# Rows sorted by pair of experts: one send, tiles of both experts, residual and norm on the sorted rows, one scatter to the output

## The reference

```python
logits = jnp.einsum('btd,ed->bte', x, Wr)
probs = jax.nn.softmax(logits / TEMPERATURE, axis=-1)
topk_vals, topk_idx = jax.lax.top_k(probs, TOPK)                  # TOPK = 2
router_weights = topk_vals / topk_vals.sum(-1, keepdims=True)
gate = jnp.einsum('btk,btke->bte', router_weights, one_hot)
h = jax.nn.silu(jnp.einsum('btd,efd->btef', x, W1))               # W1: 8 x 512 x 128
y = jnp.einsum('btef,edf->bted', h, W2)                           # W2: 8 x 128 x 512
out = jnp.einsum('bte,bted->btd', gate, y)
...
x = _layernorm(x + out, axis=-1)
```

## Time and profile before

| | us |
|---|---|
| three timed runs | 1376.46, 1378.03, 1380.54 |
| median | 1378.03 |
| the profiled execution, its own time | 1379.32 |
| its span, first to last instruction | 1377.4 |
| end of cross attention, about | 748 |
| first scatter issued / last scatter issued | 800.26 / 961.8 |
| first and last matmul of the experts | 845.34 / 1329.86 |

### The profile page before, as it was taken

One profiled execution on the slowest core, in us unless ns is written; L12 is line 12 of the kernel. 1 busy time (PEld: TensorE's weight loads), 2 busy tenths in 40 slices (PEclk: granted clock), 3 DMA queues, 4 the chain that ended last, 5 costly groups with the idle time before them and its releaser, 6 DMA issues.

```text
span 1377.4 us, 30644 instructions
## 1 busy us (share of the span) xinstructions
PE 962.4 (70%) x10082; PEld 815.0 (59%) x10083; DVE 857.2 (62%) x2598; ACT 729.5 (53%) x1364; POOL 445.7 (32%) x535
## 2 busy tenths in 40 slices
PE   4888888884999999999997402111698977676740
PEld 2777777773888888888886301000587866555530
DVE  3688888885788888888885730000454666566552
ACT  3666766653776767767763300000575765555531
POOL 3123333332010010010102357777002055654555
PEclk8989998887999999999997555555799999899985
DMA  6930000000001000000000002111233334443431
GB/s 193 290 87 15 15 15 15 15 9 18 13 11 21 10 11 17 10 19 10 0 1 1 1 38 71 51 59 52 55 93 86 92 95 106 99 107 99 101 87 53
DMA packets 157233, 73.72 MB, mean 54 GB/s; under 512 B 76034, under 2 KB 151042, under 8 KB 157188
## 3 DMA queue, kind: packets, MB, share of 16 engines
q1 hardware_dynamic: 148996, 56.34, 15.6%
q0 software_dynamic: 8192, 16.79, 4.2%
HBM read 22.76 MB, written 37.75 MB: 44 GB/s over the span
## 4 chain that ended last, share of the span: by engine, by line
PE 38%; DVE 22%; issue 21%; ACT 13%; another core or an unknown queue 2%; POOL 2%; DMA 1%; DVEq 1%; ACTq 0%; SPq 0%; POOLq 0%
PE bank L449 9%; PE bank L451 8%; PE bank L450 8%; PE bank L551 4%; DVE at L925 4%; DVE X L1002 3%; ACT XTa L746 3%; DVE mx L909 3%; ACT qzh L746 3%; PE bank L537 3%; PE bank L528 2%; DVE st L992 2%; ACT vz_self L755 1%; DVE z L937 1%
## 5 line engine op out<-in xcount | busy, mean ns | idle before, releaser
L424 POOL DMA_INDIRECT wst<-yd,pos x128 | 129.9, 1015 | 222.2 <-DVE z L1117 105.6
L449 PE MATMUL bank<-XTa,qzh 128*128 128x128 f16 x768 | 146.0, 226 | 37.7 <-ACT XTa L746 37.7
L925 DVE TENSOR_TENSOR at<-bank,rc 64x32 f32<-64x32 f32 (+1 forms) x768 | 153.5, 200 | 14.4
L831 ACT ACTIVATE pr<-bank 128x512 f32<-128x512 f32 x96 | 57.3, 597 | 192.4 <-remote 106.5
L760 ACT ACTIVATE pr<-bank 128x512 f32<-128x512 f32 x192 | 114.1, 594 | 79.5 <-PE bank L528 78.3
L909 DVE TENSOR_REDUCE mx<-bank 128x8 bf16<-128x512 f32 x192 | 132.9, 692 | 28.7 <-PE bank L451 23.1
L451 PE MATMUL bank<-XTa,qzl 128*128 128x128 f16 x768 | 146.5, 226 | 0.0
L450 PE MATMUL bank<-XTa,qzh 128*128 128x128 f16 x768 | 146.3, 226 | 0.0
L764 ACT ACTIVATE pt<-bank 128x512 f32<-128x512 f32 x192 | 113.3, 590 | 60.5 <-PE bank L537 60.1
L411 POOL DMA_INDIRECT xd<-XTa,pos x128 | 123.8, 968 | 65.3 <-issue 65.3
L1098 DVE TENSOR_TENSOR xtl<-xs,xth 128x512 f16<-128x512 f32 x96 | 66.4, 695 | 120.4 <-ACT xth L832 71.5
(11 more groups left out here) (202 smaller groups left out, 3084.5 us busy)
## 6 DMA issues: line engine op xcount, KB each, us to landing
yd<-at SPq DMA_DIRECT2D x96, 128.0 KB
xd<-blank SPq DMA_DIRECT2D x2, 3072.0 KB, 20.7
X<-x_dram SPq DMA_DIRECT2D x16, 256.0 KB, 2.8
wst<-w_dram SPq DMA_DIRECT2D x16, 256.0 KB, 2.7
xd<-blank SPq DMA_DIRECT2D x1, 4096.0 KB, 28.3
cin<-ctx_in_dram SPq DMA_DIRECT2D x16, 256.0 KB, 2.8
out_dram<-z SPq DMA_DIRECT2D x16, 256.0 KB
xd<-blank SPq DMA_DIRECT2D x1, 2048.0 KB, 21.5
```

The costliest lines, as they stand in the source:

```text
L424: nc.gpsimd.indirect_dma_start(out=yg[k][:, t, :], out_offset=None, in_=yd[chunk_of(n)], in_offset=bass.IndirectOffsetOnAxis(ap=pos[k][:, ...
L449: nc.tensor.matmul(out_, lh, rh, start=start, stop=False, **kw)
L831: nc.scalar.activation(s32[n % 4][:], bank[n % 4][:], ACT.Silu, scale=IWS)
L925: m = nc.vector.tensor_tensor(dst, src, r, ALU.mult)
```

## The change

Each row has an unordered pair of experts, one of 28. Rows are now sorted by pair, not by expert, into 92 tiles of 128 rows (64 full ones and room for 28 remainders, rounded up to a multiple of four). A row is sent once, with its two gates and its token number behind it (264 halves, 528 bytes). Each tile is put through both experts of its pair: `up` and `down` take an expert index e in place of the half c, with four hidden blocks each and 128 rows moving. The results of both experts lie in one PSUM bank; DVE adds them, times the gates that travelled along, onto the residual row that POOL rebuilt from its halves (`mix`), takes the statistics, and POOL applies the norm and scatters the rows straight to the output by token number (`give`); padding rows carry the number 8192 and are dropped. The stores to yd, the gathers, the four chunks, DVE's copies, ACT's share of the norm and the last 13 groups' finish behind PE are gone. SP waits for all 64 sends before its first load.

The core of the diff:

```diff
+PAIRS = [(a, b) for a in range(E) for b in range(a + 1, E)]
+NP = len(PAIRS)
+NTILE = 4 * ((TOK // P + NP - 1 + 3) // 4)
+PB = NP // 4 * NT
+ROW = 2 * D + 8
...
+            for n in range(NT // SEG):
+                sp.wait_ge(sent[n], 16 * SEG)
...
-                for t in range(t0, t1):
-                    for k in range(2):
-                        nc.gpsimd.indirect_dma_start(out=xd[chunk_of(t)], out_offset=bass.IndirectOffsetOnAxis(ap=pos[k][:, t:t + 1], axis=0),
-                                                     in_=xhl[:, t, :], in_offset=None).then_inc(sent[n], 16)
+            for t in range(NT):
+                if t % SEG == 0 and t >= 2 * SEG:
+                    pool.wait_ge(sent[t // SEG - 2], 16 * SEG)
+                nc.gpsimd.indirect_dma_start(out=xd, out_offset=bass.IndirectOffsetOnAxis(ap=pos[:, t:t + 1], axis=0),
+                                             in_=rows_out[:, t, :], in_offset=None).then_inc(sent[t // SEG], 16)
+            def take(j, i):
+                wait_apart(pool, ld_r[i], 8 * (j - i) + 16, pool_ready, POOL_READY)
+                nc.gpsimd.tensor_tensor(zr[i], row16[i][:, :, 0:D], row16[i][:, :, D:2 * D], ALU.add).then_inc(f_xs, 1)
+                nc.gpsimd.tensor_copy(held[:, i, :], row_token[i]).then_inc(f_id, 1)
+            def give(j, i, more):
+                inv_std(j, f_ag, 2 * G, f_rs)
...
+                    nc.gpsimd.tensor_scalar(zo[k], zr[i][:, k, :], mv[:, k, 0:1], rstd[:, k:k + 1], ALU.subtract, ALU.mult).then_inc(f_fin, 1)
...
+                for k in range(4):
+                    nc.gpsimd.indirect_dma_start(out=out_rows, out_offset=bass.IndirectOffsetOnAxis(ap=dest[:, k:k + 1], axis=0), in_=zo[k],
+                                                 in_offset=None, bounds_check=TOK - 1, oob_is_err=False).then_inc(put[k], 16)
+                if more:
+                    take(j + 2, i)
...
-            def up(k, c, base):
-                n = 2 * (k % 2) + c
-                for h in range(2):
-                    w = base + (2 * c + h) * 2 * P
-                    m = three(H[n][:, h * RT:(h + 1) * RT], (W1[:, bass.ds(w, P)], W1[:, bass.ds(w + P, P)]),
+            def up(q, e, base):
+                r = slice(q % 2 * P, q % 2 * P + P)
+                for f in range(FC):
+                    w = base[e] + f * 2 * P
+                    m = three(H[(2 * q + e) % 4][:, f * P:(f + 1) * P], (W1[:, bass.ds(w, P)], W1[:, bass.ds(w + P, P)]),
...
-                    for r in range(2):
-                        q = slice(h * RT + r * P, h * RT + (r + 1) * P)
-                        m = three(Y[k % 2][:, r * P:(r + 1) * P], (sh[n][:, q], sl[n][:, q]), (W2[:, bass.ds(w, P)], W2[:, bass.ds(w + P, P)]),
+                for f in range(FC):
+                    w = base[e] + f * 2 * P
+                    c = slice(f * P, (f + 1) * P)
+                    m = three(Y[q % 4][:, e * P:(e + 1) * P], (sh[n][:, c], sl[n][:, c]), (W2[:, bass.ds(w, P)], W2[:, bass.ds(w + P, P)]),
...
+            nc.vector.tensor_tensor(M16.rearrange("p (c t) -> p c t", t=NT), rt[:, 0].unsqueeze(1).to_broadcast([P, NP, NT]),
+                                    code.unsqueeze(2).to_broadcast([P, NP, NT]), ALU.is_equal).then_inc(r_m, 1)
...
+            for n in range(4):
+                b = slice(n * PB, (n + 1) * PB)
+                dve.wait_ge(r_rank, n + 1)
+                link(nc.vector.tensor_tensor_scan(runs[:, b], wipe[:, b], bank[4 + n][:, 0:PB], 0.0, ALU.mult, ALU.add))
...
+                link(nc.vector.tensor_tensor(runs[:, b], runs[:, b], bank[n][:, 0:PB], ALU.add))
...
+            link(nc.vector.scalar_tensor_tensor(out=runs_c, in0=start.unsqueeze(2).to_broadcast([P, NP, NT]), scalar=float(P), in1=runs_c,
+                                                op0=ALU.mult, op1=ALU.add))
+            link(nc.vector.tensor_tensor(runs, runs, M16, ALU.mult))
+            link(nc.vector.tensor_reduce(rt[:, 0], runs.rearrange("p (c t) -> p t c", t=NT), AX.X, ALU.add))
...
+            def mix(i, q, e):
...
+                nc.vector.scalar_tensor_tensor(out=z4, in0=bank[4 + q % 4][:, e * P:(e + 1) * P], scalar=row_gate[q // 4][:, q % 4, e:e + 1],
+                                               in1=z4, op0=ALU.mult, op1=ALU.add).then_inc(f_z if e else f_a, 1)
```

More of the change, by code:

```diff
@@ L316, in _ @@
+            for n in range(NT // SEG):
+                sp.wait_ge(sent[n], 16 * SEG)
+            for k in range(2):
+                load(k, k)
+            load_rows(0, 0)
+            for k in range(2, 4):
+                load(k, k)
+            load_rows(1, 1)
+            turn(0, 0)
+            with sp.Fori(0, (NJ - 3) // 2) as j:
+                turn(2 * j + 1, 1)
+                turn(2 * j + 2, 0)
         @block.gpsimd
@@ L427, in _ @@
[L427 to L441 removed]
+            pool.wait_ge(r_id, 1)
@@ L444, in _ @@
+            nc.gpsimd.memset(dest[:], 0).then_inc(f_fin, 4)
+            take(0, 0)
+            take(1, 1)
+            give(0, 0, True)
+            with pool.Fori(0, (NJ - 3) // 2) as j:
+                give(2 * j + 1, 1, True)
+                give(2 * j + 2, 0, True)
+            give(NJ - 2, 1, False)
+            give(NJ - 1, 0, False)
+            for k in range(4):
+                pool.wait_ge(put[k], 16 * NJ)
         @block.tensor
@@ L692, in four @@
                         if follow:
[L693 to L696 removed]
+                            up((q + 1) % 8, e, ahead)
+                        if k == 1 and e == 0 and not last:
+                            pe.reg_mov(pairs, load_word(j + 1))
+                        down(i, q, e, base)
                     base = ahead
[L699 to L700 removed]
@@ new lines, in _ @@
+            runs_c = runs.rearrange("p (c t) -> p c t", t=NT)
+            nc.vector.tensor_scalar(over[:], runs_c[:, :, NT - 1], lane_rows, None, ALU.is_gt).then_inc(r_ov, 1)
+            dve.wait_ge(r_ov, 1)
+            for n in range(4):
+                b = slice(n * PB, (n + 1) * PB)
+                link(nc.vector.tensor_tensor(runs[:, b], runs[:, b], bank[n][:, 0:PB], ALU.add))
+            dve.wait_ge(r_nt, 1)
+            nt, cum, start, ones_c = (small[:, n * NP:(n + 1) * NP] for n in range(4))
@@ new lines, in turn @@
+                    if k == 2 and not start:
+                        dve.wait_ge(f_ag, j)
+                    if k > 1 or not start:
+                        spread(i - 2, (q + 6) % 8)
+                    if k > 0 or not start:
+                        mix(i - 1, (q + 7) % 8, 1)
+                    if k == 1 and not start:
+                        moments(j - 1)
+            turn(0, 0)
+            with dve.Fori(0, (NJ - 1) // 2) as j:
+                turn(2 * j + 1, 1)
+                turn(2 * j + 2, 0)
```

451 lines of the change are left out of this document (174 added, 277 removed).

## The result

| | before | after |
|---|---|---|
| median of 11 runs, us | 1381.05 | 1371.4 |
| lowest to highest, us | 1376.46 to 1390.51 | 1365.83 to 1374.14 |
| span of the profiled execution, us | 1377.4 | 1366.2 |

The ratio is 0.9907 (95% interval 0.9884 to 0.9929): 0.9% faster, just clear of what can't be told from nothing. The forecast was 1377, its own range 1362 to 1392. But the time came about differently than forecast, and the kernel before turned out to have two times, 1381 and 1226, depending on the chip that it ran on.

What follows compares the result with a forecast made beforehand. PE's sequencer was taken to bound the expert loop: 896.1 + 23 x 19.2 = 1337.7, plus 23 stutter, 13 tail, 2.5 slow start and clock = 1376.3; adjusted for time outside the span and run offset, 1377 us, range 1335 to 1425.

Steps and rivals of the forecast that it cites:

- stutter in the loop: Expert loop: PE's issue gaps behind each turn's burst of four scatters, 1.05 us for 22 bursts, +23, bounds 0 to 47.
- slow start, clock: Expert start and loop: 1.5 us for PE's slow start plus 1 for the granted clock, +2.5 in all.
- Router and sends: Before the experts: router +10.3 us, first scatter at 810.6, 64 scatters 1.266 apart, first matmul at 896.1.
- The turn: Expert loop: four tiles, set by PE's sequencer, 64 more address instructions at 0.124 us, 19.2 for 11.46 us.
- the ring: Loop, from the experiments: DVE's moments, POOL's inverse deviation, norm and scatters, then rebuilt rows DVE waits for; 15.2 us.
- Rival C: Expert loop: address instructions are cheaper and hide beneath the matmuls, turn 11.7 us, 1205 in all; chance 0.10.
- The stutter: PE while POOL issues indirect transfers: single matmuls 1.4 us apart in the sends, with waits marked issue.
- rival B: Expert loop: no stutter, four scatters a turn never outlast what PE holds, 1354 us (1345 to 1361); chance 0.20.
- a stock of 137 instructions: Expert loop: what PE has in hand when a burst starts, lasting 4.2 us before the change and 4.9 after.
- The tail: From PE's last matmul to the end: weighing to norm 4.1, norms 1.5, scatters 5.1, landing 2.2; 13 for 47.5 us.
- Rival D: Expert loop: 2.15 us of stutter a burst and 1.2 GHz for half the loop, 1417 us (1393 to 1440); chance 0.20.
- 120 us of stutter during the sends: Kernel before, 852.43 to 976.00: PE hardly moves while POOL sends, so its early start was judged of little use.

Runs made afterwards that it cites:

- The wide down: Kernel after with high and low half of W2 as one 256-column moving operand, 96 instead of 128 address instructions a turn: 1293.24 us, ratio to before 0.9372.
- constant addresses: Kernel after with weights of experts 1 and 2 at constant addresses: 1276.15 us; with POOL's rebuilding also ahead of the scatters, on another chip: 1232.04.
- two bursts close together: Kernel after with four extra transfers a turn ahead of POOL's norm: gathers 1406.14 us; scatters 1391.66, and 1400.36 on another chip.
- eight in a row: Kernel after with four more scatters of the same rows into a spare buffer directly behind each turn's four: 1453.87 us.
- the second group: Runs made together on another chip, where the unedited kernel before took 1226.17 us; with SP waiting for all 128 sends it took 1350.22.
- relative with the extra scatters: Kernel after with four extra scatters into a spare buffer ahead of POOL's norm each turn: 1391.66 us there, 1400.36 on another chip.
- The wide kernel with the early rebuilding: Kernel after with 256-column W2 operand, POOL rebuilding rows before the scatters, DVE norming the last four tiles: 1277.92 us there, 1285.37 on another chip.
- the kernel after's three relatives: Kernel after with extra scatters (1391.66 us); with wide down and early rebuilding (1277.92); with constant addresses and early rebuilding (1232.04).

## Why the prediction was right, point by point

The sum of 1376.3 for the span and the 1366.2 measured differ by these terms, all in us:

| step | forecast | measured | difference |
|---|---|---|---|
| first matmul (router, sends) | 896.1 | 893.6 | -2.5 |
| 23 turns, first to last matmul | 441.6 | 448.3 | +6.7 |
| stutter in the loop | 23 | 0 | -23 |
| slow start, clock | 2.5 | 0 | -2.5 |
| last matmul to the end | 13 | 24.3 | +11.3 |

**Router and sends** were right: the first scatter came 7.8 us later than before for the forecast 10.3, since the chain from the comparison with the pairs to the places took 21.5 us for some 24, and rows of 528 bytes cost as much POOL time as those of 512 (962 ns both).

**The turn** was right in its mechanism and 2% short: 19.58 for 19.2. The wide down took 32 address instructions out and the turn, once the ring was open, fell by 19.58 - 15.6 = 4.0, 0.124 each, just as the prediction had read off the spacing in the earlier trace rows. (The 15.6 are from the chip without stutter; with it they are 16.0.) Rival C is out.

The Trainium skill, TensorE: Matmul & The Clock Gate, section Back-to-back issue gap, gives about 81 ns for a weight load with a 128-column matmul. This case does not agree: with constant addresses and no stall these ran 56 ns apart (12 in 0.67 us).

**The stutter** was the step that failed. Forecast at 1.05 a burst, it was nothing on PE in the kernel after, and rival B had this mechanism right. The assumption was a stock of 137 instructions, used up after 4.9 us. The runs give no single stock: gaps began 4.2 us behind the start before, 2.9 to 4.8 with constant addresses, 5.1 with two bursts close together, and mostly 8 with eight in a row. A burst of four scatters keeps POOL busy for 5.3 us in the loop. So why PE gets through it in the kernel after is not shown. That B's time of 1354 was missed is the doing of the tail and of the longer turns. None of the theories had ACT, whose delays the slow sequencer hides here.

**The tail** was sized too small. A norm of 128 columns on POOL costs 0.79, not a quarter of the 1.51 for 512: 3.1 for 1.5. Between the copy and the first scatter lie 0.9 us of POOL's own register work, and behind the last lies the drain of 8.9, which the prediction did not have; in the kernel before it was 1.6.

So the errors of -28 and +18 nearly cancel, and that is luck: with only the tail sized right, the forecast would have been 1388. The forecast time was right, the road to it half right.

**Rival D** did not come: the clock in the loop was 1.00 though the array stood still 45% of the time. In the run with constant addresses it did fall, from 1000 to 1200 us each time while PE stood in a wait of 4.4 us.

What the prediction did not have was the chip. It charged the kernel before with 120 us of stutter during the sends as if that were the kernel's own. On the chip of the second group the kernel before takes 1226 without it. The kernel after was not run there. Its relative with the extra scatters had there, up to the eleventh, turns of 19.2 to 20.3 us, each within 0.1 of the kernel after's own, so by the sum it should take about 1366 there and be 11% slower than the kernel before; this is argued, not shown. The wide kernel with the early rebuilding, which beats both on the other chips (1285 against 1381 and 1371), is 4.2% slower there (ratio 1.0423, 1.038 to 1.0467).

## What to carry to other kernels

Count a dynamic address as work of the matrix engine's sequencer, 0.124 us each: work split into smaller matmuls with an address for each can leave the array idle for half of its time while the profile calls it 91% busy. Making one operand twice as wide so that two products share an address was worth 4 us in 19.6. And before an overlap is written off because an engine crawls in it, have the kernel timed on more than one chip: what looked like a property of the schedule was one of the place it ran in. Look at every engine's starts behind what it waits for, too: a view of the engine that limits the kernel shows nothing of a delay that a faster kernel will meet.

## What the runs showed of the hardware that was not expected

- The same kernel before took 1381, 1383 and 1381 us on three chips and 1226 us on a fourth, each time in all of 7 to 13 runs. PE's stutter was in the traces from two of the three (on the third only kernels that hardly meet it were traced), ACT's late starts in those from all three. The traces from the fourth have no stutter of PE, and those of the kernel after's three relatives there no late start of ACT. Whether it is the chip or where the program was placed in it can't be told from these runs.
- Where there is a stutter, PE stutters in steps of 0.7 and 1.4 us while POOL issues indirect transfers, gathers or scatters alike, also in a loop; this started 2.9 to 8 us behind the first of them. ACT started up to 7.4 us late there, with eight scatters in a row.
- POOL's closing drain took 8.9 us in programs with 156 indirect transfers and 1.6 in those with 256.
- On POOL, subtracting the mean and multiplying by the inverse deviation took 0.79 us for 128 columns, where a product over 512 columns took 1.51.
